# Edge ranks by a looked-up bucket start and a comparison of a lane's 16 tiles, in place of a prefix scan, in a two-layer graph network

## What is computed

```python
h = lrelu(node_features @ w_W + w_b)
edge_h = lrelu(edge_features @ ew_W + ew_b)
e_ij = concatenate([h[tgt], h[nbr], edge_h], axis=-1) @ a_W + a_b
alpha = segment_softmax(e_ij, tgt)          # over all edges of a target
out = lrelu(segment_sum(alpha * h[nbr], tgt))
```

## Time and profile before

| | us |
|---|---|
| median of 3 runs | 5,577.67 (5,574.44 to 5,582.21) |
| span of the profiled execution | 5,576.0 |
| PE busy in the span | 4,012.4 (72%) |
| DVE busy | 3,670.6 (66%) |
| POOL busy | 3,626.7 (65%) |
| ACT busy | 2,032.7 (36%) |
| DMA | 679.76 MB, mean 122 GB/s |

### The profile page before, as it was taken

The page is one execution under the profiler, slowest core; times in us unless marked ns, Lnnn a source line. Parts: engine busy times, 40 slices in busy tenths (PEclk is TensorE's granted clock), DMA queues, the critical chain, the costliest instruction groups (busy, mean ns, idle before and its releaser), DMA issues. The chain is left out here.

```text
span 5576.0 us, 86962 instructions
## 1 busy us (share of the span) xinstructions
PE 4012.4 (72%) x18762; PEld 3066.0 (55%) x18763; DVE 3670.6 (66%) x11238; ACT 2032.7 (36%) x5477; POOL 3626.7 (65%) x3655
## 2 busy tenths in 40 slices
PE   5488888888888888888888736666666666666662
PEld 3366666666666666666666525555555555555551
DVE  8777777777777777777777545555555555555554
ACT  0243433434333343333433213333333333333334
POOL 0477666666666666666666337777777777777773
PEclk9799998999999999999999868888888888888886
DMA  1355555555555555555555434444444434444433
GB/s 42 105 154 152 140 144 147 140 149 139 143 148 141 146 141 143 146 143 147 139 143 146 78 108 106 106 106 106 106 107 106 106 106 106 106 106 106 106 106 65
DMA packets 544286, 679.76 MB, mean 122 GB/s; under 512 B 340246, under 2 KB 376430, under 8 KB 543996
## 3 DMA queue, kind: packets, MB, share of 16 engines
q0 software_dynamic: 174144, 469.02, 32.0%
q1 hardware_dynamic: 355132, 196.63, 13.2%
q10 hardware_dynamic: 14976, 13.69, 0.7%
HBM read 650.32 MB, written 27.79 MB: 122 GB/s over the span
## 5 line engine op out<-in xcount | busy, mean ns | idle before, releaser
L612 POOL DMA_INDIRECT rows<-in_x,picked x1785 | 1823.1, 1021 | 960.4 <-issue 543.7
L1468 POOL DMA_INDIRECT room<-nodetab,nbr_idx x1736 | 1642.8, 946 | 562.4 <-issue 487.6
L645 PE MATMUL bank<-w_edge,feats 128*128 128x258 f32 x3264 | 1067.9, 419 | 441.4 <-ACT bank L781 426.1
L660 PE MATMUL bank<-rows,hot 128*128 128x320 f32 x3570 | 1328.2, 474 | 9.4 <-DMA rows<-in_edge 6.4
L1498 PE MATMUL bank<-room,w 128*128 128x258 f32 x3472 | 1033.8, 461 | 55.6 <-ACT w L1544 54.9
L1530 ACT ACTIVATE w<-off,logit 128x128 f32<-128x128 bf16 x1736 | 534.0, 388 | 1359.6 <-DVE logit L1582 1359.6
L645 PEld LDWEIGHTS bank<-w_edge,feats 128*128 128x128 f32 x3264 | 608.2, 208 | 666.2 <-ACT bank L781 509.0
L1498 PEld LDWEIGHTS bank<-room,w 128*128 128x128 f32 x3472 | 798.6, 237 | 250.3 <-ACT w L1544 102.7
L1015 DVE SCALAR_TENSOR_TENSOR unused<-bank,a_relu 128x258 bf16<-128x258 f32 x1632 | 682.3, 420 | 316.8 <-PE bank L645 312.6
L1489 PE MATMUL bank<-ident,w 128*128 128x128 f32 x1736 | 298.7, 323 | 782.2 <-ACT w L1530 782.2
L660 PEld LDWEIGHTS bank<-rows,hot 128*128 128x128 f32 x3570 | 748.8, 210 | 187.4 <-issue 40.8
(11 more groups left out here) (314 smaller groups left out, 4484.4 us busy)
## 6 DMA issues: line engine op xcount, KB each, us to landing
feats<-in_edge SPq DMA_DIRECT2D x408, 256.0 KB
rows<-in_edge SPq DMA_DIRECT2D x255, 128.0 KB, 2.9
rows<-in_x,picked POOLq DMA_INDIRECT x1785, 3.0
room<-nodetab,nbr_idx POOLq DMA_INDIRECT x1736
rows<-in_edge SPq DMA_DIRECT2D x153, 160.0 KB, 3.3
nodetab<-tab ACTq DMA_DIRECT2D x52, 129.0 KB, 3.2
x_blk<-in_x SPq DMA_DIRECT2D x52, 128.0 KB, 2.1
x_rows<-u_n ACTq DMA_DIRECT2D x52, 128.0 KB
```

Of the source, the lines that this page charges most:

```text
L612: pool.indirect_dma_start(out=rows[:, STARTS[j] + s, 0:D], out_offset=None, in_=a["x"], in_offset=bass.IndirectOffsetOnAxis(ap=picked[j][: ...
L645: mm(y, feats[:, f0 * P:(f0 + 1) * P], w_edge[:], start=False, stop=True, skip_group_check=True).then_inc(o["y_ready"], 1)
L660: ins = mm(S_PS, hot[j % HR][:, s - STARTS[j], :], rows[:, s, :], start=(s == 0), stop=(s == SA - 1), skip_group_check=True)
L1468: pool.indirect_dma_start(out=nbr[:, u * GC + k, :], out_offset=None, in_=nodetab, in_offset=bass.IndirectOffsetOnAxis(ap=nbr_idx[u][:, k: ...
```

## The change

The rank is computed as a sum of two parts per edge, held side by side in `parts`, [tile, 50 + 16]: the edge's one-hot times the starts of its group's buckets (`look_up`), and a one for each of the lane's 16 tiles that has the same bucket and doesn't come later (`in_lane`, `up_to_here` with the constant `not_after`). `halve`, `halve_again` and `rank_of` add the 66 cells. `find` writes `hb` directly, from the doubled bucket numbers `hi_two`, which now live on into this stage; `hf`, `keep`, `upto`, `iota_bt` and ACT's `narrow` are gone. `totals` folds `hb` over tiles, `triangle` is two matmuls of 100 columns in place of four of 49, and `keep_triangle` is one copy. `find` moves from kk = 4 to 3, `totals` to 4 to 6, `rank_pairs` to 17, `slots` to 18, 21, 23, 27 and `tag_keys` from 20, 22, 24 to 19, 25, 29.

```diff
...
@@ -479,11 +479,14 @@
             unused = sb("unused", [P, EB, D + 2], BF16, ctx)
             a_relu = sb("a_relu", [P, D + 2], F32, ctx)
             r_cur = sb("r_cur", [P, TILES], F32, ctx)
-            hf = sb("hf", [P, NB * U, L + 1], BF16, ctx)
-            keep = sb("keep", [P, NB * U, L + 1], BF16, ctx)
-            upto = sb("upto", [P, NB * U, L + 1], BF16, ctx)
-            iota_bt = sb("iota_bt", [P, NB, TILES], BF16, ctx)
-            fold = sb("fold", [P, NB * U, L // 2], BF16, ctx)
+            fold = sb("fold", [P, U, L // 2, NBP], BF16, ctx)
+            starts = sb("starts", [P, U, NBP], BF16, ctx)
+            not_after = sb("not_after", [P, L, L], BF16, ctx)
+            parts = sb("parts", [P, TILES, NBP + L], BF16, ctx)
+            HALF = (NBP + L) // 2
+            half = sb("half", [P, TILES, HALF], BF16, ctx)
+            assert HALF % 2 == 1
+            few = sb("few", [P, TILES, HALF // 2 + 1], BF16, ctx)
             hb = sb("hb", [P, TILES, NBP], BF16, ctx)
             rank = sb("rank", [P, TILES], BF16, ctx)
             rank_two = sb("rank_two", [P, TILES, 2], BF16, ctx)
@@ -666,9 +669,8 @@
                     pe.wait_ge(o["tot_ready"], p + 1)
                     pe.wait_ge(o["tri_kept"], p)
-                    for u in range(U):
-                        for n in range(2):
-                            ins = mm(TRI[:, u * NB:(u + 1) * NB], below_bf[:], fold[:, u::U, n], start=(n == 0), stop=(n == 1))
+                    for n in range(2):
+                        ins = mm(TRI, below_bf[:], fold[:, :, n, :], start=(n == 0), stop=(n == 1))
                     ins.then_inc(o["tri_ready"], 1)
                 def sort(w, u, tiles):
@@ -780,19 +782,9 @@
                     act.wait_ge(o["logit_ready"], p * TILES + (kk - EB + 1 + LOG0))
                     s.copy(banks[kk % EB][:, 0:D + 2], b_edge[:]).then_inc(o["seeded"], 1)
-                def narrow(p):
-
-                    act.wait_ge(o["hf_ready"], p + 1)
-                    act.wait_ge(o["tagged_ready"], p + 1)
-                    for u in range(U):
-                        ins = s.copy(hb[:, u * L:(u + 1) * L, 0:NB], hf[:, u::U, 1:L + 1].rearrange("p b t -> p t b"))
-                    ins.then_inc(o["hb_ready"], 1)
-
                 def keep_triangle(p):
                     act.wait_ge(o["tri_ready"], p + 1)
-                    for u in range(U):
-                        ins = s.copy(hf[:, u::U, 0], TRI[:, u * NB:(u + 1) * NB])
-                    ins.then_inc(o["tri_kept"], 1)
+                    s.copy(starts[:].rearrange("p u b -> p (u b)"), TRI).then_inc(o["tri_kept"], 1)
                 def pack(w, u):
                     act.wait_ge(o["sorted"], w * U + (u + 1))
@@ -854,8 +846,6 @@
                             keep_triangle(p)
                         if kk in node:
                             node[kk](p)
-                        if kk == 6:
-                            narrow(p)
                 act.wait_ge(o["primed"], 1)
                 for kk in range(AHEAD):
@@ -915,53 +903,52 @@
                 def find(p, at):
-                    dve.wait_ge(o["tri_ready"], p)
-                    v.tensor_tensor(hf[:, :, 1:L + 1].rearrange("p (b u) t -> p b u t", u=U),
-                                    hi_f[:, bass.ds(at, TILES)].rearrange("p (u t) -> p u t", u=U).unsqueeze(1).to_broadcast([P, NB, U, L]),
-                                    iota_bt[:].rearrange("p b (u t) -> p b u t", u=U), ALU.is_equal).then_inc(o["hf_ready"], 1)
+                    wait_alone(dve, (o["tagged_ready"], p + 1))
+                    v.tensor_tensor(in_pairs(hb[:]), pairs_over(iota_b[:], TILES), over_pairs(hi_two[:, bass.ds(at, TILES), :], NBP),
+                                    ALU.is_equal).then_inc(o["hb_ready"], 1)
                 def totals(p, n):
-                    wide = L // 2 >> n
+                    many = L // 2 >> n
                     if n == 0:
-                        wait_alone(dve, (o["hf_ready"], p + 1))
-                        low, high = hf[:, :, 1:wide + 1], hf[:, :, wide + 1:L + 1]
+                        wait_alone(dve, (o["hb_ready"], p + 1))
+                        by_group = hb[:].rearrange("p (u t) b -> p u t b", u=U)
+                        low, high = by_group[:, :, 0:many, :], by_group[:, :, many:L, :]
                     else:
                         wait_alone(dve, (o["folded"], p * 2 + n))
-                        low, high = fold[:, :, 0:wide], fold[:, :, wide:2 * wide]
-                    v.tensor_tensor(fold[:, :, 0:wide], low, high, ALU.add).then_inc(o["folded" if n < 2 else "tot_ready"], 1)
-
-                SCANS = tuple(NB * U * n // 4 for n in range(5))
-
-                def scan(p, n):
-                    if n == 0:
-                        wait_alone(dve, (o["tri_kept"], p + 1))
-                    flat, piece = "p b t -> p (b t)", slice(SCANS[n], SCANS[n + 1])
-                    v.tensor_tensor_scan(upto[:, piece, :].rearrange(flat), keep[:, piece, :].rearrange(flat), hf[:, piece, :].rearrange(flat),
-                                         0.0, ALU.mult, ALU.add).then_inc(o["scanned"], 1)
-
-                def mask(p, n):
-                    wait_alone(dve, (o["scanned"], p * 4 + (n * 2 + 2)))
-                    piece = slice(SCANS[n * 2], SCANS[n * 2 + 2])
-                    v.tensor_tensor(upto[:, piece, 1:L + 1], upto[:, piece, 1:L + 1], hf[:, piece, 1:L + 1], ALU.mult
-                                    ).then_inc(o["masked"], 1)
-
-                HALF_NB = NB - NB // 2
-                FOLDS = ((0, NB // 2, HALF_NB), (0, HALF_NB // 2, HALF_NB - HALF_NB // 2))
-                LEFT = HALF_NB - HALF_NB // 2
-
-                def fold_blocks(p, n):
-                    wait_alone(dve, (o["masked"], p * 4 + n + 2))
-                    lo, many, hi = (U * m for m in FOLDS[n])
-                    v.tensor_tensor(upto[:, lo:lo + many, 1:L + 1], upto[:, lo:lo + many, 1:L + 1], upto[:, hi:hi + many, 1:L + 1],
-                                    ALU.add).then_inc(o["masked"], 1)
+                        low, high = fold[:, :, 0:many, :], fold[:, :, many:2 * many, :]
+                    v.tensor_tensor(fold[:, :, 0:many, :], low, high, ALU.add).then_inc(o["folded" if n < 2 else "tot_ready"], 1)
+
+                def in_lane(p, u, at):
+                    pairs = hi_two[:, bass.ds(at + u * L, L), :]
+                    v.tensor_tensor(in_pairs(parts[:, u * L:(u + 1) * L, NBP:NBP + L]), pairs_over(hi_f[:, bass.ds(at + u * L, L)], L),
+                                    over_pairs(pairs, L), ALU.is_equal).then_inc(o["paired"], 1)
+
+                def up_to_here(p, u):
+                    wait_alone(dve, (o["paired"], p * (2 * U) + (u + U - 1)))
+                    seen = parts[:, u * L:(u + 1) * L, NBP:NBP + L]
+                    v.tensor_tensor(seen, seen, not_after[:], ALU.mult).then_inc(o["paired"], 1)
+
+                def look_up(p, u):
+                    if u == 0:
+                        dve.wait_ge(o["tri_kept"], p + 1)
+                    v.tensor_tensor(parts[:, u * L:(u + 1) * L, 0:NBP], hb[:, u * L:(u + 1) * L, :],
+                                    starts[:, u, :].unsqueeze(1).to_broadcast([P, L, NBP]), ALU.mult).then_inc(o["looked"], 1)
+
+                def halve(p):
+                    wait_alone(dve, (o["looked"], p * U + U), (o["paired"], p * (2 * U) + 2 * U))
+                    v.tensor_tensor(half[:], parts[:, :, 0:HALF], parts[:, :, HALF:2 * HALF], ALU.add).then_inc(o["halved"], 1)
+
+                def halve_again(p):
+                    wait_alone(dve, (o["halved"], p * 2 + 1))
+                    v.tensor_copy(few[:, :, HALF // 2:HALF // 2 + 1], half[:, :, HALF - 1:HALF])
+                    v.tensor_tensor(few[:, :, 0:HALF // 2], half[:, :, 0:HALF // 2], half[:, :, HALF // 2:HALF - 1],
+                                    ALU.add).then_inc(o["halved"], 1)
                 def rank_of(p):
-                    wait_alone(dve, (o["masked"], p * 4 + 4))
+                    wait_alone(dve, (o["halved"], p * 2 + 2))
                     with nc.allow_low_precision(reason="one whole number; those over 128 only have to stay over it"):
-                        v.tensor_reduce(rank[:].rearrange("p (u t) -> p u t", u=U),
-                                        upto[:, 0:LEFT * U, 1:L + 1].rearrange("p (b u) t -> p u t b", u=U), AX.X, ALU.add
-                                        ).then_inc(o["ranked"], 1)
+                        v.tensor_reduce(rank[:], few[:], AX.X, ALU.add).then_inc(o["ranked"], 1)
                 def rank_pairs(p):
                     wait_alone(dve, (o["ranked"], p * 2 + 1))
@@ -1126,28 +1113,32 @@
                         edge(p, kk)
                         if kk < 3:
                             tag_logits(p, kk)
-                        if kk == 4:
+                        if kk == 3:
                             find(p, at)
-                        if 5 <= kk < 8:
```

(31 more changed lines are left out.)

12 lines of the change are left out of this document (5 added, 7 removed).

## The result

| | before | after |
|---|---|---|
| median, us | 5,578.9 (5,574.4 to 5,582.2) | 5,342.5 (5,340.6 to 5,342.6) |
| span of the profiled execution, us | 5,576.0 | 5,338.8 |
| ratio after/before | | 0.9575 (0.9562 to 0.9588) |

One more execution of the kernel after was a slow one, 6,119.8 us at a mean granted clock of 0.66 against 0.89, and isn't counted here.

What follows compares the result with a forecast made beforehand. No engine is full; PE stalls three times a pass on ACT's late seeds, and its clock drops behind two. 58.0 - 1.26 - 3.5 + 1.1 = 54.4 us a pass, 185 us less over 51 passes: 5,393 us, range 5,310 to 5,490.

Steps and rivals of the forecast that it cites:

- A: PE's stall ahead of edge tile 8, behind ACT's two copies into hb; 1.26 us a pass, forecast to go.
- B: PE's 3.42 us stall ahead of tile 26, behind ACT's square root awaiting out_norm's mv; forecast 1.47 less, 1.95 left.
- The clock behind B is up: PE's clock after the shortened B stays at 1.00 instead of 0.50, giving back 2.8 us a pass.
- `table` held by DVE's list: From mv to table DVE's list takes 8.4 us, so table starts 3.5 us earlier, not 4.3; C grows 0.8.
- C: PE's 3.90 us stall ahead of tile 2 of the next pass, its seed behind ACT's wait for table; forecast 0.8 longer.
- 1.1 us more of low clock behind C: After a longer C the low clock may last longer: bounds 0 and 1.1 us a pass, 1.1 taken.
- The triangle: ACT's two small copies become one and PE's four matmuls two; costed at nothing, not over 0.3 us.
- rival 2: No low clock after B, and C or its low stretch no longer than now: 5,337 to 5,297 us; 15%.
- Rival 1: The clock falls after B all the same: 55.3 us a pass, 5,439 us; 22%.
- a 0.5 there: Sign in the changed profile: granted clock behind B at 0.5 instead of the forecast 1.00 means Rival 1.
- Rival 3: New DVE instructions cost what the old did, or something unseen holds out_norm; only ACT's copy is won: 5,514 us; 8%.
- Rival 4: POOL becomes the bound as its gathers take longer: 59.0 us a pass, 5,629 us, slower; 3%.

Runs made afterwards that it cites:

- f3: Kernel after with two ACT copies of the old kind put back at tile 6, between tiles nobody else uses; 5,415.2 us, ratio 0.9705.
- e7: Kernel after with two more DVE products of 1,600 elements at tiles 13 and 15, ahead of the second and third residual; 5,341.4 us.
- e6: Kernel after with two more DVE products of 1,600 elements at tiles 19 and 21, between the third residual and out_norm; 5,470.3 us.
- f2: Kernel before with DVE writing hb at tile 3 in place of ACT's two copies, scans left; 5,465.7 us, ratio 0.9791.
- e8: Kernel after with DVE's list rearranged: tag_keys at 17 and twice at 31, slots at 23, 24, 26, 28; 5,251.5 us, ratio 0.9406.
- e5: Kernel after with one more DVE product of 1,600 elements at tile 19, between the third residual and out_norm; 5,411.4 us.

## Why the prediction was right, and where its sizes were off

- **The three stalls and ACT's list.** Right. A is gone and comes back with two copies on ACT (f3, 1.27 us against 1.26).
- **B, 1.47 us less, left at 1.95.** Right: 1.96. That DVE's work behind the third `residual` counts, and that ahead of it doesn't, is shown by e7 against e6.
- **The clock behind B is up, 2.8 us back.** Right in 24 of 41 passes only. In 17 it is low for 3.4 us, so that 2.25 us a pass come back. The forecast took one stall to have one outcome, from the nearer of two rows.
- **`table` held by DVE's list, C grows by 0.8.** Right in mechanism: DVE needs 8.47 us from `mv` to `table` (8.4 forecast) and waits for PE for 0.2 of them in the pass shown. Where the clock stays up behind B, C grows by 0.7, near the forecast; where it doesn't, by 0.07, since PE is later too. The mean is 0.4.
- **1.1 us more of low clock behind C.** This is the term that was most mis-sized: the low clock behind C costs 0.16 us more. It was a choice from bounds of 0 and 1.1, made for the reason that a longer C might be followed by a longer low stretch. It was longer in 7 of 41 passes. The upper bound was taken without a row that asked for it.
- **The triangle**, costed at nothing (not over 0.3): 0.25 us.
- **The sum.** Stalls 2.25 us against 1.26 + 1.47 - 0.8 = 1.9 forecast, the clock 2.1 against 2.8 - 1.1 = 1.7, the triangle 0.25 against nothing, and 0.25 unsettled: 4.9 against 3.6. The clock's two terms were off by 0.55 and 0.9 us with opposite signs, so that its sum came out nearer than either deserved; that part is luck. So is how near the steady pass of 53.15 us and the time of 5,342 come to the end of rival 2, 53.3 and 5,337: that rival had no low clock behind B at all.
- **Rival 1**, a low clock behind B all the same: by the prediction's own sign, a 0.5 there, it holds in 17 of 41 passes, at a cost of 1.7 us in each and not 2.8, and it is what happens in all passes of e6, at 3.46. As the whole story (55.3 us a pass) it is refuted.
- **Rival 3**, only the ACT copy is won, 5,514 us: its cause is refuted by the durations above. Its price was off too: f2, which is that rival built, took 5,465.7, with a shorter low stretch behind B in 28 of 40 passes.
- **Rival 4**, POOL becomes the bound: not here. A gather took 1,019 ns on the mean before and 1,006 after. In e7, with two products more a pass, it took 1,041, so 35 gathers cost 1.2 us more, in POOL's waiting time:

```profile
L615 POOL DMA_INDIRECT rows<-in_x,picked x1661 | 1671.2, 1006 | 681.9 <-issue 550.6 <-DVE picked L1009 120.4 <-PE bank L663 10.4
```

```profile
L616 POOL DMA_INDIRECT rows<-in_x,picked x1660 | 1728.8, 1041 | 633.4 <-issue 594.5 <-DVE picked L1010 26.5 <-PE bank L664 12.2
```

- The Trainium skill (GPSIMD Engine Reference, Specifications) names DVE instructions with two SBUF inputs as what shares GpSimd's interfaces; the direction agrees with both rows, and the rate that they show, 35 ns a gather for 1.97 us of such work a pass, is far from what rival 4 needed.
- **DVE's new instructions.** 4.41 us against 4.4. `halve`, whose second half starts at element 33, takes 0.735 us, as the rate of aligned ones has it (0.71), and not 1.2. The Trainium skill (VectorE: DVE Perf Modes, Mode 2×_1P) asks for 4-byte alignment; this row speaks against it, and for its Vector Engine (DVE) Microarchitecture Reference, 5.1.
- **The setup.** 0 to 0.4 us was right in kind: the memsets' time is lost in the wait for the weights, which is 6.00 us now, for 0.40.

```profile
200.31 0.42 DVE L889 CUSTOM_DVE_ANT_0 hot<-w_edge,rows 128x256 f32<-128x256 f32 x1 [6.00 <-DMA b_mlp<-in_mlp_b]
```

- **Left out of the forecast**: that the ends of the loop gain less than its middle. The last two passes gain 3.5 and 1.5 us for 4.9, and 1.7 us are given back behind them: small against 51 passes, but counted as nothing.

## What to carry to other kernels

Follow a stall back through the in-order list of the engine that releases it, to the last point at which that list itself waited; only work behind that point shortens the stall, and what is moved ahead of it is free (e7, e8). Where TensorE's clock drops behind a stall, the stall has a second price of up to nearly its own size (3.0 us on 3.4 here). It shrinks as the stall gets shorter: 0.7 us a pass at 1.96 us, nothing at 0.9 (e8), so the first microseconds taken off are worth more than the later ones. Read the clock over all passes, not in one: here the pass first looked at had no low clock behind B, and two passes on there was one. Where an unknown has two ends and no row asks for the dear one, let the forecast stand on the nearer row, reckon that a part of the passes may go the other way, and keep the other end for the range.

## What the runs showed of the hardware

The same stall in the same place is followed by a low clock in one pass and not in the next. TensorE's granted clock, over the steady passes of each kernel:

| stall B, us | kernel | passes | clock stays at 1.00 | 0.50 for 3.4 us | 0.50 for 6.8 us |
|---|---|---|---|---|---|
| 0.82 to 0.94 | e8 | 42 | 42 | 0 | 0 |
| 1.96 | after | 41 | 24 | 17 | 0 |
| 1.95 | e7 | 41 | 25 | 16 | 0 |
| 1.95 | f3 | 40 | 25 | 15 | 0 |
| 2.38 to 2.45 | e5 | 40 | 34 | 6 | 0 |
| 3.38 to 3.46 | f2 | 40 | 0 | 28 | 12 |
| 3.41 to 3.47 | e6 | 39 | 0 | 26 | 13 |
| 3.38 to 3.42 | before | 38 | 0 | 0 | 38 |

Stall A, 1.26 us, left the clock at 1.00 in the passes shown (before, f3). Behind C, 3.90 us in the kernel before and 3.96 to 4.73 after, it was low in every pass. PE's work just behind B is the same in all of them, so neither the stall's length nor that work alone decides whether the clock falls and for how long; what else does wasn't tested. A sum that takes the low clock behind a stall from one pass can be off by about 1 us a pass, as f2's was.
